# A DLRM interaction tower on one core: the transposes of the gathered rows go from TensorE to DMA

## The reference, cut to what matters

```python
e = jnp.stack([tbl_0[ids[:, 0]], ..., tbl_25[ids[:, 25]]], axis=1)
all_emb = jnp.concatenate([bottom_output[:, None, :], embeddings], axis=1)
gram = jnp.einsum('bfd,bgd->bfg', all_emb, all_emb)
z = gram[:, _TRIU_I, _TRIU_J]
h = jnp.concatenate([z, r_bottom_output], axis=1)
h = jnp.maximum(h @ W_top1 + b_top1, 0.0)      # 479 x 512
h = jnp.maximum(h @ W_top2 + b_top2, 0.0)      # 512 x 256
y = h @ W_top3                                 # 256 x 1
```

## Time and profile before

| | us |
|---|---|
| median of 3 runs (lowest, highest) | 382.97 (382.36, 384.99) |
| profiled execution, its own time | 382.43 |
| span of the profiled execution, first to last instruction | 380.7 |
| TensorE busy | 348.3 |
| VectorE busy | 261.8 |
| ScalarE busy | 117.8 |
| GpSimd busy | 263.8 |

### The profile page before, as it was taken

One profiled execution on the slowest core, in us unless ns is written; L12 is line 12 of the kernel. 1 busy time (PEld: TensorE's weight loads), 2 busy tenths in 40 slices (PEclk: granted clock), 3 DMA queues, 4 the chain that ended last, 5 costly groups with the idle time before them and its releaser, 6 DMA issues.

```text
span 380.7 us, 14045 instructions
## 1 busy us (share of the span) xinstructions
PE 348.3 (91%) x6112; PEld 311.4 (82%) x6112; DVE 261.8 (69%) x781; ACT 117.8 (31%) x218; POOL 263.8 (69%) x281
## 2 busy tenths in 40 slices
PE   0879869999998999989998999989999899999997
PEld 0767759898887999978887898978998799887886
DVE  4999998985757957566537866677767586723232
ACT  3453641333223322313232341313323133132311
POOL 5777777777777777777777777777777777775000
PEclk9999998999999999999999999999999899999999
DMA  7755574332242312212331322413123212121000
GB/s 229 198 148 205 173 236 163 94 85 55 54 97 58 92 51 57 79 50 59 98 92 50 94 54 54 106 51 91 50 58 99 57 50 57 52 57 46 4 2 1
DMA packets 16684, 32.42 MB, mean 85 GB/s; under 512 B 5488, under 2 KB 8176, under 8 KB 16496
## 3 DMA queue, kind: packets, MB, share of 16 engines
q0 software_dynamic: 8704, 17.84, 18.4%
q1 hardware_dynamic: 7920, 13.69, 11.6%
HBM read 31.50 MB, written 0.01 MB: 83 GB/s over the span
## 4 chain that ended last, share of the span: by engine, by line
PE 80%; DVE 15%; DMA 3%; issue 1%; ACT 1%; SPq 0%; ACTq 0%; DVEq 0%
PE hot_ps L366 36%; DVE onehot L496 11%; PE gram_ps L346 11%; PE h_ps L407 10%; PE h_ps L419 8%; PE xt_ps L329 7%; PE h_ps L404 5%; DVE tab L545 3%; DMA stage_sb<-in_hot_dram 3%; PE zt_ps L385 2%; DVE h L535 1%; PE hot_ps L407 0%; ACT tab L633 0%; DMA ids_wide<-in_hot_ids_dram 0%; DVE Z L504 0%
## 5 line engine op out<-in xcount | busy, mean ns | idle before, releaser
L318 POOL DMA_INDIRECT X<-in_table_dram,rows_sb x272 | 262.4, 965 | 84.3 <-issue 81.1
L496 DVE TENSOR_SCALAR onehot<-ids_wide,row_value 128x256 fp32r<-128x256 int16 x640 | 199.5, 379 | 81.4 <-PE hot_ps L366 78.5
L366 PE MATMUL hot_ps<-onehot,tab 128*128 128x256 f32 x1280 | 191.9, 298 | 13.7 <-DVE onehot L496 13.5
L366 PEld LDWEIGHTS hot_ps<-onehot,tab 128*128 128x128 f32 x1280 | 166.7, 194 | 20.4 <-issue 13.3
L475 ACT COPY XT<-xt_ps 128x512 f32<-128x512 f32 x64 | 38.9, 608 | 165.2 <-PE xt_ps L329 165.2
L346 PEld LDWEIGHTS gram_ps<-XT 128*27 128x27 f32 x4096 | 40.6, 105 | 23.1 <-issue 14.8
L346 PE MATMUL gram_ps<-XT 128*27 128x26 f32 x4096 | 53.5, 190 | 4.4 <-DVE Z L504 3.2
L604 ACT COPY XT<-hot_ps 128x256 f32<-128x256 f32 x72 | 49.4, 686 | 25.1 <-PE hot_ps L366 24.7
L407 PE MATMUL h_ps<-stage_sb,w_sb 128*128 128x256 f32 (+3 forms) x198 | 45.1, 363 | 0.0
L329 PE MATMUL xt_ps<-ident,X 128*128 128x128 f32 x272 | 40.8, 272 | 2.1 <-ACT XT L471 1.9
L419 PE MATMUL h_ps<-w_sb,stage_sb 128*128 128x256 f32 x128 | 32.9, 402 | 9.3 <-DVE h L535 9.3
(11 more groups left out here) (32 smaller groups left out, 59.6 us busy)
## 6 DMA issues: line engine op xcount, KB each, us to landing
ids_wide<-in_hot_ids_dram SPq DMA_DIRECT2D x14, 320.0 KB
X<-in_table_dram,rows_sb POOLq DMA_INDIRECT x272
stage_sb<-in_hot_dram SPq DMA_DIRECT2D x15, 256.0 KB, 4.2
stage_sb<-in_hot_dram SPq DMA_DIRECT2D x10, 192.0 KB, 3.1
bottomT<-in_bottom_t_dram SPq DMA_DIRECT2D x8, 128.0 KB, 4.1
w_sb<-in_w_dram SPq DMA_DIRECT2D x1, 1024.0 KB
w_sb<-in_w_dram SPq DMA_DIRECT2D x1, 512.0 KB, 9.2
vec_sb<-in_vecs_dram SPq DMA_DIRECT2D x1, 256.0 KB, 9.3
```

What stands on the lines that cost most here:

```text
L318: pool.indirect_dma_start(X[:, n % RING, k, :], None, table, bass.IndirectOffsetOnAxis(idx[:, column:column + 1], 0)).then_inc(gathered[n ...
L366: mm = pe.matmul(hot_ps[i % 2][:, 0:WIDE], tab[u][:, part, D * c:D * (c + 1)], onehot[p % ONEHOTS][:, c - PIECE[u][h], :], start=(c == 0 a ...
L496: compared = dve.tensor_scalar(onehot[p % ONEHOTS][:, c - PIECE[u][h], :], ids_wide[:, u, :], row_value[:, c:c + 1], None, ALU.is_equal)
```

## The change

TensorE's transposes go. A unit takes another way: ACT copies the four gathered squares, read as 16-bit words, into `planes`, low words apart from high words (`split_words`, one instruction of 128x1024 words); SP issues one DMA that transposes the eight 128x128 squares of words to `turned` (`turn`); ACT puts the two halves back together in XT with two copies of 128x512 words (`move_xt`). Planes and turned hold two units each. ACT separates the unit of block b+3 at the end of its block b (AHEAD = 3). X holds four units (RING = 4), freed by the separating. HOTS is 6 for the first pair and 10 for the seven others: 66 units, 264 gathers, 1,360 products in place of 1,280 and 680 one-hots in place of 640. The turns stand in SP's queue between the loads; for blocks 1 to 3 (EARLY = 4) the turn of block b stands behind the table pieces that block b-1 casts and ahead of those that block b casts. Layer 3 of a pair stands earlier in DVE's order (behind the first one-hot of the block), and the last pair has an order of its own (`last_step`): its layers stand between its Gram products and not behind them.

```diff
-RING = 7
+RING = 4
+TURNED = 2
+AHEAD = 3
+EARLY = 4
-HOTS = [HOT_BASE, HOT, HOT, HOT, HOT_BASE, HOT, HOT, HOT]
+HOTS = [HOT_BASE] + [HOT] * (GROUPS - 1)
...
+            def turn(n):
+                sp.wait_ge(planes_ready, n + 1)
+                wait(sp, xt_moved, n - TURNED + 1)
+                sp.dma_start_transpose(turned[:, n % TURNED, :, :], planes[:, n % TURNED, :, :, :].rearrange("p k h d -> p (k h d)")
+                                       ).then_inc(turned_in[n % TURNED], 16)
...
             load_low_ids(1)
+            turn(0)
+            turn(1)
+            load_high_ids(1)
             for q in range(FIRST_PIECE[HOT_BASE], FIRST_PIECE[HOT_BASE + 1]):
                 load_piece(q)
-            load_high_ids(1)
-            for q in range(FIRST_PIECE[HOT_BASE + 1], FIRST_PIECE[HOT]):
-                load_piece(q)
+            for b in range(1, EARLY):
+                for n in UNITS_OF[b]:
+                    turn(n)
+                for q in range(FIRST_PIECE[HOT_BASE + b], FIRST_PIECE[HOT_BASE + b + 1]):
+                    load_piece(q)
             load_bottom(1)
             load_bottom(2)
             sp.dma_start(w1_sb[:], w1).then_inc(w1_in, 16)
             sp.dma_start(w2_sb[:], w2).then_inc(w2_in, 16)
             sp.dma_start(vec_sb[:], row_vecs.to_broadcast([P, 2, N2])).then_inc(vecs_in, 16)
-            for n in range(2, GROUPS):
-                load_low_ids(n)
-                load_high_ids(n)
-                if n >= BOTTOMS // 2:
-                    load_bottom(n)
+            for b in range(EARLY, TILES * BLOCKS):
+                for n in UNITS_OF[b]:
+                    turn(n)
+                n = b // (2 * BLOCKS)
+                if b % (2 * BLOCKS) == 0 and 2 <= n + 1 < GROUPS:
+                    load_low_ids(n + 1)
...
-                wait(pool, xt_full, n - RING + 1)
+                wait(pool, planes_ready, n - RING + 1)
...
+            def last_step(b):
...
+                if b == TILES * BLOCKS - BLOCKS + 2:
+                    gram_block(b)
+                    layer1(len(JOBS) - 2, 0)
...
+                    layer2(TILES - 3)
+                if b == TILES * BLOCKS - 1:
+                    layer2(TILES - 2)
+                    gram_block(b)
...
             eng.wait_ge(turned_in[n % TURNED], 16 * (n // TURNED + 1))
...
+                for h in range(2):
+                    moved = copy(words[:, t % XTILES, PAD * j:PAD * (j + 1), 0:ALWAYS, h].rearrange("d s (k f) -> d s k f", f=FOUR),
+                                 turned[:, n % TURNED, h::2, :].rearrange("d k (s f) -> d s k f", f=FOUR))
...
+            def split_words(b):
+                for n in UNITS_OF.get(b, []):
+                    act.wait_ge(gathered[n % RING], 16 * FOUR * (n // RING + 1))
+                    if n >= TURNED:
+                        act.wait_ge(turned_in[n % TURNED], 16 * (n // TURNED))
+                    act.copy(planes[:, n % TURNED, :, :, :],
+                             X[:, n % RING, :, :].bitcast(i16).rearrange("p k (d h) -> p k h d", h=2)
+                             ).then_inc(planes_ready, 1)
...
                 for i in ended(b):
                     place_hot(i)
...
+                for q in LATE_PIECES[PER_STEP * b:PER_STEP * (b + 1)]:
+                    split_first(q)
+                if b < TILES * BLOCKS - 1 - AHEAD:
+                    split_words(b + AHEAD)
+                if b == TILES * BLOCKS - 3:
+                    split_words(b + 2)
...
-    nc = _bacc.Bacc("TRN2", target_bir_lowering=False, num_devices=1, dynamic_dma_scratch_size=4096)
+    nc = _bacc.Bacc("TRN2", target_bir_lowering=False, num_devices=1, dynamic_dma_scratch_size=2048)
```

More of the change, by code:

```diff
@@ L36 @@
 RUNS = 2
+SPLIT_STEPS = 4
 GROUPS_PER_BANK = 16
@@ L177, in build @@
         bottom_placed = sem("bottom_placed")
-        xt_full = sem("xt_full")
+        planes_ready = sem("planes_ready")
+        turned_in = [sem(f"turned_in{s}") for s in range(TURNED)]
         xt_moved = sem("xt_moved")
@@ L323, in _ @@
         def _(pe):
[L324 to L330, removed]
             def gram(b, run):
@@ L449, in step, with gram_block @@
                 mlp(b // BLOCKS, b % BLOCKS)
+            def last_step(b):
+                j = b % BLOCKS
+                if b < TILES * BLOCKS - BLOCKS:
+                    gram_block(b)
+                    mlp(b // BLOCKS, j)
+                if b == TILES * BLOCKS - BLOCKS:
+                    gram_block(b)
+                    layer1(len(JOBS) - 3, 2)
+                    layer1(len(JOBS) - 3, 3)
+                if b == TILES * BLOCKS - BLOCKS + 1:
+                    gram_block(b)
+                    z_transposes(TILES - 2)
+                    layer2(TILES - 4)
+                if b == TILES * BLOCKS - BLOCKS + 2:
+                    gram_block(b)
+                    layer1(len(JOBS) - 2, 0)
+                    layer1(len(JOBS) - 2, 1)
+                    layer1(len(JOBS) - 2, 2)
+                    layer1(len(JOBS) - 2, 3)
+                    layer2(TILES - 3)
+                if b == TILES * BLOCKS - 1:
+                    layer2(TILES - 2)
+                    gram_block(b)
+            def gram_block(b):
+                for run in range(RUNS):
+                    gram(b, run)
             pe.wait_ge(ident_ready, 1)
@@ L454, in _ @@
                 lookups(0, PRODUCTS[0][u], PRODUCTS[0][u + 1])
-                if u >= 3 and u - 3 in UNITS_OF[0]:
-                    transposes(u - 3)
-            for b in range(TILES * BLOCKS):
+            for b in range(LAST):
                 step(b)
+            for b in range(LAST, TILES * BLOCKS):
+                last_step(b)
             z_transposes(TILES - 1)
-            layer2(TILES - 2)
             for c in range(C1):
@@ L553, in step @@
                     move_zt(t - 1)
-                for p in pieces_ended(b):
+                freed = pieces_ended(b)
+                for p in freed[:1]:
+                    one_hot(p + ONEHOTS)
+                if t >= 3 and t % 2 == 1 and j == 3 and t < TILES - 1:
+                    layer3(t - 3)
+                if t == TILES - 1 and j >= 2:
+                    layer3(t - 5 + j)
+                for p in freed[1:]:
                     one_hot(p + ONEHOTS)
@@ L557, in step @@
                     fold(t - 1)
[L558 to L563, removed]
+                for q in LATE_PIECES[PER_STEP * b:PER_STEP * (b + 1)]:
+                    split_second(q)
                 if t >= 4 and t % 2 == 0 and j == 0:
@@ L647, in step @@
                 relus(t, j)
+                if b == TILES * BLOCKS - 2:
+                    relu(len(JOBS) - 2, 0)
+                    relu(len(JOBS) - 2, 1)
                 moves(b + 1)
+                if b == TILES * BLOCKS - 2:
+                    relu(len(JOBS) - 2, 2)
+                    relu(len(JOBS) - 2, 3)
                 for i in ended(b):
@@ L665, in _ @@
                     place_hot(u - 1)
-                if u >= 4 and u - 4 in UNITS_OF[0]:
-                    move_xt(act, nc.scalar.copy, u - 4)
+                if u == HOT_BASE - 2:
+                    split_words(0)
+            moves(0)
             place_hot(HOT_BASE - 1)
@@ L670, in _ @@
             place_bottom(0)
+            for b in range(1, AHEAD):
+                split_words(b)
             for b in range(TILES * BLOCKS):
```

37 lines of the change are left out of this document (21 added, 16 removed).

## The result

| | us |
|---|---|
| before, median of 4 runs (lowest, highest) | 382.67 (382.06, 384.99) |
| after, median of 4 runs (lowest, highest) | 395.38 (394.99, 396.36) |
| ratio after/before, 95% interval | 1.0325 (1.0276 to 1.0373) |
| span of the profiled execution, before and after | 380.7, 394.5 |

The change costs 3.3%.

What follows compares the result with a forecast made beforehand. TensorE was taken to bound the kernel, with gathers a close next limit. Span 380.7 + 28.1 (start) - 17.6 (body) + 7.2 (last pair) = 398.4, with 1.7 us around it 400 us; range 366 to 430.

Steps and rivals of the forecast that it cites:

- The start: Up to block 4's first Gram product: turns not hidden, so it comes at 84.3 in place of 56.24, +28.1 us.
- The three orders: At the start: ACT moves before casting, the load awaiting a cast piece precedes the next turn, and the move needs that turn.
- The turn: One transposing DMA of 256 KB on SP: lands in 4.2 us like a plain load, hidden in the steady state.
- rival C: Turn dearer than a load: 426 us at a 6 us landing, 443 at 7, 574 at 11.2; chance 0.26.
- rival B: Start half covered: turns of 3.1 us pass the weights in the queue, block 4 at 70.6, time 385; chance 0.08.
- ACT: ACT's new work: separating a unit 1.1 us, a move 1.38 us, some 3.7 of 5.2 us a block, no bound by itself.
- the prediction's own last sentence: Wrong if the turn takes under 3 or over 6 us, lands ahead of earlier weights, or ACT's stages aren't 1.1 and 1.4.
- The body: Block 4 to 56: -22.7 for transposes, +9.6 for 80 more products, -9.1 for layer 3, +4.6 for late DVE: -17.6 us.
- early layer 3: In the body: the second layer's wait for layer 3 goes, five waits, -9.1 us.
- the transposes: TensorE in the body: 54 units save 0.42 us each, -22.7 us; DVE late in six pairs, +4.6.
- The last pair: Block 56 to the end: blocks wait for gather, separating, turn and move; 43.0 us in place of 35.8, +7.2.
- Rival A: Start covered, only gathers bind, time 366; kernel faster where block 4 is late by less than 10.5 us; chance 0.19.

Runs made afterwards that it cites:

- Experiments 1 to 3: Changed kernel with weights issued behind the turns of blocks 4 to 10: 393.31 us; turns of blocks 2 to 4 one load group earlier: 385.48; both: 380.49.
- experiment 4: Changed kernel with layer 3 back behind the block's other work on DVE, at six places before the last pair: 411.9 us, 1.0805 of before.
- the kernel with the orders and the old last pair: Changed kernel with weights behind the turns, turns one load group earlier, and the old order of the last pair: 375.43 us, 0.9782 of before.
- experiment 6: Changed kernel with the old order of the last pair: 392.18 us; the same with weights behind the turns and turns one load group earlier: 375.43 us.
- experiment 3: Changed kernel with weights behind the turns of blocks 4 to 10 and turns of blocks 2 to 4 one load group earlier: 380.49 us, 0.9938 of before.
- experiment 2: Changed kernel with the turns of blocks 2 to 4 one group of table loads earlier in SP's queue: 385.48 us, 1.0067 of before.

## Why the prediction was right

The forecast was 400 us, the time is 395.4. It came out through the right steps at the start, through a sum in the body whose total was right and whose parts are not settled, and through a wrong step in the last pair. That the last pair's size came out (43.0 us booked, 44.3 seen) is luck.

**The start: right, and 3.6 us too much.** The three orders meet as traced. The turn of block 4 goes out at 64.50 (booked 65.3) behind the vectors, and lands at 72.45 (76.3). ACT waits 11.0 us for it (13), and block 4 starts at 80.73 (84.3). GpSimd waits for ACT 11.4 us there (9.9 and 1.5), less than the 15 to 25 of the forecast; its 26.8 us are those of the whole span. The term that was mis-sized is the landing behind the weights: I took the 9.2 and 9.3 us of the earlier trace rows, and the weights now land in 6.5 to 7.5. Experiments 1 to 3 show that most of it is order: at block 4 moving the weights gives 6.4 us, moving the turns 16.0, both 17.4. The 7.1 us that are left were not taken apart.

**The turn: right.** Booked 4.2 us, seen 4.93, 4.48, 3.36 and, in the last pair, 4.61; so rival C (6 us and more) is out. Only the turn behind the weights is longer, 7.95 us, and that it lands behind them takes rival B out too. The body hides the turns: the moves wait for them 30.5 us in 21 waits over the whole span, on ACT, which is busy for 60%, while TensorE is busy for 265.5 of the body's 270.4 us. The Trainium skill's page "DMA: Bandwidth & Descriptors", section "Latency and other measured facts", led to a landing like that of a plain load, and the trace agrees (3.4 to 4.9 beside 3.5 for a load of 256 KB). The Trainium skill's page "VectorE: DVE Perf Modes", section "The three transpose paths", read as eight squares in a row gave 10.5 us; the trace doesn't agree with that reading.

**ACT: right in sum.** Separating 1.07 us (1.1). A move is two copies of 0.88, some 1.6 us as a pair in the timeline, where I had 1.38 from the placings; the upper bound of 2.0 holds. By the prediction's own last sentence a move of another time than 1.4 us was a sign of being wrong; it is 0.2 us off. That cost little in the body, where TensorE idles for 4.9 us in all; in the start and in the last pair the moves stand in the chain.

**The body: right in sum.** -19.1 us beside -17.6. By parts: early layer 3 alone -11.1 (booked -9.1), the seventh pair alone +8.5 (+9.6), which leaves -16.5 for the transposes with all that comes of them (booked -22.7 + 4.6 = -18.1). This last number is a difference, and no run had the transposes alone. The parts do not simply add, either: taken out of the changed kernel (experiment 4), early layer 3 is worth 15.2 us of body, and by that only 12.4 would be left for the transposes. What the prediction's -9.1 leaves out is the busy time that goes with the waits: 3.2 us of the 11.1 here, 5.4 of the 15.2 there.

**The last pair: right size, wrong cause.** I wrote that each block waits "for gather, separating, turn and move in ACT's order". ACT waits for no gather: no such row is among the waits of the kernel after (the same view does show 0.5 us of it in the kernel with the orders and the old last pair). The last gather starts at 358.7, and the last unit is separated only at 370.1. What fails is the step that priced the new order of the layers as a gain (13.1 us behind block 63 in place of 15.2) and put the loss on gathers that come late. By experiment 6 the order costs 6.1 us of the 8.5: it gives back 1.0 us behind block 63 and loses 7.1 ahead of it. What remains, 2.4 us beside before, is in the blocks with turns; I saw ACT's waits for turns and moves there, but ran nothing on them alone.

**Rival A** asked for block 4 late by less than 10.5 us. In experiment 3 it is late by 7.1, and the kernel is 0.6% faster than before; in experiment 2 it is late by 8.5, and the kernel is 0.7% slower. So the turning point lies between the two and not at 10.5. A's time of 366, the gathers' bound, lay far from any run, since TensorE bounds the body.

**The best version** is the kernel before with layer 3 early, 373.1 us, 2.7% under before, run beside it, and 5.6% under the median of after, which was not run beside it. The transposing DMA with both orders and the old last pair comes to 375.4, and that holds early layer 3 too: over that part alone the rest of the change still costs 2.3 us by medians, with its orders mended, though the intervals of the two ratios overlap (0.9729 to 0.9835 and 0.968 to 0.9779). The seventh pair of lookups is in it, which costs 7.7 us by itself; the transposing DMA with the mended orders and the old HOTS was not run.

## What to carry to other kernels

When a step is moved from an engine to a DMA, write down the one queue that issues it, with everything ahead of it and what that waits for; here the loads and waits ahead of a 4 to 5 us transfer cost 17.4 us, and none of them had to stand there. Before moving work out of an engine at its limit, look for short waits behind work that can stand elsewhere in a written order: layer 3 moved on DVE gave 9.8 us and took no work or buffer, and part of the gain was a clock that no longer fell behind the waits. When a run is to decide between two causes, ask first what each would show: in experiment 3 both gave the same last pair, since its start moved with its gathers. Work put ahead of the last product must fill a gap there; where it was, it filled the gap behind it.

## What the runs showed of the hardware that was not expected

- The granted clock fell in the start. With waits of 3.5 us between lookups it was 0.60 of 2.4 GHz from 48 to 60 us and, around one of 10.1 us, 0.54 from 70 to 80.6, near the lower level of 1.2 GHz, and 11 lookups took 2.72 us at 60.98 where they take 1.57 in the earlier trace rows. In the body it was 0.99. In the last pair, behind a wait of 1.88 us for a move, the first part of layer 1 took 2.77 us at 357.78 and the next, at 361.82, 1.46. Waits of 2 us were enough in experiment 4, but not each time: behind the five in the body the second layer took 3.3 to 3.6 us three times and 1.99 twice.
- A turn of 128x1024 words of 16 bits (256 KB) holds SP's queue for 1.23 us, where issuing a weight load takes 0.43, and with the 66 turns SP's queue has 77,616 packets and 42.4% of the 16 DMA engines' time, in place of 7,920 and 11.6% before. The gathers' 0.94 us didn't change beside it.
- A copy of 128x512 words of 16 bits that stores every second word takes 876 ns on ACT, where 512 words of 32 bits to the same slots take 608; separating 1024 such words takes 1074 ns.
